# One-core linear-attention and gated-FFN kernel: the first two steps reordered, and chunk 0's first norm divided among three engines

## The reference

```
a   = layernorm(x)
q   = a @ Wq + bq                        # 16 heads of 16
k,v = (a @ Wk + bk) @ Wc @ We, (a @ Wv + bv) @ Wc @ We   # 4 heads, each used by 4 heads of q
qf, kf = elu(q) + 1, elu(k) + 1
o   = (qf . cumsum(kf v^T)) / (qf . cumsum(kf) + EPS)    # causal linear attention
y   = a + (o @ Wo + bo)                  # residual inside the attention block is a
x2  = x + (layernorm(y) * gamma + beta)  # the "first norm" of the change
z   = layernorm(x2)                      # the "second norm"
out = x2 + sigmoid(mix(z, mu_r) @ Wr^T) * (relu(mix(z, mu_k) @ Wk^T)^2 @ Wv^T)
```

## Time and profile before

| | us |
|---|---|
| median of 3 runs | 285.71 |
| lowest and highest of them | 284.47 and 287.39 |
| the profiled execution | 283.59 |
| span of the profiled execution (first to last instruction) | 281.9 |

### The profile page before, as it was taken

One profiled execution on the slowest core, in us unless ns is written; L12 is line 12 of the kernel. 1 busy time (PEld: TensorE's weight loads), 2 busy tenths in 40 slices (PEclk: granted clock), 3 DMA queues, 4 the chain that ended last, 5 costly groups with the idle time before them and its releaser, 6 DMA issues.

```text
span 281.9 us, 7526 instructions
## 1 busy us (share of the span) xinstructions
PE 262.1 (93%) x2961; PEld 188.8 (67%) x2961; DVE 219.6 (78%) x540; ACT 155.7 (55%) x316; POOL 137.9 (49%) x163
## 2 busy tenths in 40 slices
PE   7996997996999999999999999999999899979694
PEld 7854656754875688559855887568855776756573
DVE  6578576978897889798979799786979668976523
ACT  2466685595637945586448754785158610454550
POOL 2636464398851595355832585256535322242410
PEclk9799999999999999999999999999999999999999
DMA  6910220000200040002200020002000110000312
GB/s 187 257 47 1 77 78 2 3 0 2 74 3 2 2 148 3 1 3 76 77 0 2 2 76 2 2 2 77 0 2 3 40 39 0 0 2 0 113 37 74
DMA packets 12178, 10.73 MB, mean 38 GB/s; under 512 B 2288, under 2 KB 12144, under 8 KB 12144
## 3 DMA queue, kind: packets, MB, share of 16 engines
q1 hardware_dynamic: 11392, 9.97, 11.5%
q10 hardware_dynamic: 752, 0.30, 0.4%
HBM read 6.07 MB, written 4.19 MB: 36 GB/s over the span
## 4 chain that ended last, share of the span: by engine, by line
PE 80%; DVE 9%; ACT 5%; POOL 3%; issue 3%; DVEq 0%; POOLq 0%; ACTq 0%
PE ps_x L478 10%; PE ps_x L398 9%; PE ps_x L493 6%; PE ps_x L500 6%; PE ps_z L449 6%; PE ps_x L392 6%; PE ps_y L465 6%; PE ps_y L470 6%; PE ps_x L518 4%; PE ps_z L493 3%; PE ps_z L500 2%; PE ps_x L486 2%; ACT z_tok L810 2%; PE ps_z L672 2%; PE ps_x L385 2%
## 5 line engine op out<-in xcount | busy, mean ns | idle before, releaser
L1016 DVE TENSOR_TENSOR probs<-ps_z,causal 128x1024 f32<-128x1024 f32 x32 | 38.7, 1210 | 5.5 <-PE ps_z L449 4.5
L275 POOL TENSOR_TENSOR prod<-qf,ksum 128x1024 f32<-128x1024 f32 x7 | 16.6, 2365 | 32.7 <-DVE ksum L989 32.7
L478 PE MATMUL ps_x<-wo_sb,oT 128*128 128x256 f32 x128 | 29.6, 382 | 0.0
L290 POOL TENSOR_TENSOR out_tok<-tanh_r,x_tok 128x512 f32<-128x512 f32 x14 | 17.9, 1279 | 21.9 <-DVE tanh_r L1090 20.6
L398 PE MATMUL ps_x<-aT,wq_sb 128*128 128x512 f32 x60 | 27.8, 604 | 0.0
L260 POOL TENSOR_TENSOR abo_tok<-a_tok,bo_bc 128x1024 f32<-128x1024 f32 x8 | 18.9, 2361 | 16.5 <-issue 6.8
L267 POOL TENSOR_TENSOR xb_tok<-x_in,beta_bc 128x1024 f32<-128x1024 f32 x8 | 18.8, 2354 | 15.9 <-DVE x_tok L1062 15.9
L478 PEld LDWEIGHTS ps_x<-wo_sb,oT 128*128 128x128 f32 x128 | 23.6, 190 | 3.8 <-issue 0.9
L220 POOL TENSOR_TENSOR rstd<-rstd,neg_half 128x4 f32<-128x4 f32 x24 | 24.9, 1039 | 1.9
L449 PE MATMUL ps_z<-qf,kfT 32*128 32x128 f32 x512 | 23.3, 295 | 1.9 <-ACT rden_bc L730 0.5
L465 PEld LDWEIGHTS ps_y<-qf,state 32*32 32x32 f32 x512 | 11.9, 104 | 16.8 <-issue 13.9
(11 more groups left out here) (147 smaller groups left out, 615.3 us busy)
## 6 DMA issues: line engine op xcount, KB each, us to landing
x_in<-in_L_attn_x_dram SPq DMA_DIRECT2D x8, 512.0 KB, 4.3
out_dram<-out_tok SPq DMA_DIRECT2D x16, 256.0 KB, 2.2
xr<-in_L_attn_Wq_dram ACTq DMA_DIRECT2D x1, 256.0 KB, 4.1
xk<-in_L_ffn_W_r_dram SPq DMA_DIRECT2D x1, 256.0 KB, 5.0
xk<-in_L_ffn_W_k_dram SPq DMA_DIRECT2D x1, 256.0 KB, 5.2
xr<-in_L_ffn_W_v_dram SPq DMA_DIRECT2D x1, 256.0 KB, 5.7
wo_sb<-in_L_attn_Wo_dram SPq DMA_DIRECT2D x4, 64.0 KB, 5.3
bo_bc<-in_L_attn_bo_dram SPq DMA_DIRECT2D x1, 128.0 KB, 5.0
```

The lines of the kernel that those rows point to most:

```text
L478: last = mm(bk_[:, (b % 2) * D:(b % 2 + 1) * D], oT[m % 2][:, a, b, :], wo_sb[:, a, :], start=(a == 0), stop=(a == 1))
L1016: V.tensor_tensor(probs[b % 2][:].rearrange("p g (r s) -> p g r s", s=HALF), ps_z[:, :, 0:2 * P].rearrange("p g (r s) -> p g r s", s=HALF) ...
```

## The change

In steps 0 and 1, PE makes both transposes of `a`, and in step 1 the first half of the output projection, in step 0 the first FFN weight's transposes, before `spread_reciprocals`; in step 0 `keys_values` stands ahead of `scores(0, 1)` too. ACT and DVE take the matching order (`reciprocals` after `a_out(n, 1)`; `keys_values` ahead of `mask(0, 1)` in step 0).

The first norm of chunk 0 is made row by row on two ways. Rows 0 and 1: ACT normalises, POOL multiplies by gamma and adds xb. Rows 2 and 3: DVE does `centre` and `second_residual`, placed between `mask(1, 2)` and `queries(2, 0)`. `second_stats` is one call for all four rows, between `queries(2, 0)` and `queries(2, 1)`; it waits for POOL's two rows on the new semaphore s_xg. POOL makes `second_norm(0)` ahead of `denominator_terms(2)`. The wider increments of s_t and s_x2 keep the counts of the later steps as they were.

```diff
@@ -105,7 +105,7 @@
         y_tok, z_tok = sb("y_tok", NB, D), sb("z_tok", NB, D)
         stats1, mv1, rstd1 = sb("stats1", NB, 6), sb("mv1", NB, 2), sb("rstd1", NB)
         neg_mean1, nbias1 = sb("neg_mean1", NB), sb("nbias1", NB)
-        s_nb1, s_n1 = sem("nbias1_ready"), sem("y_scaled")
+        s_nb1, s_n1, s_yg, s_xg = sem("nbias1_ready"), sem("y_scaled"), sem("y_gamma"), sem("x2_by_pool")
         stats2, mv2, rstd2, neg_mean2, nbias2 = sb("stats2", NB, 6), sb("mv2", NB, 2), sb("rstd2", NB), sb("neg_mean2", NB), sb("nbias2", NB)
         zT, dz = sb("zT", KD, NB, P + 1), sb("dz", KD, NB, P)
         xk, xr = sb("xk", KD, NB, P), sb("xr", KD, NB, P)
@@ -238,15 +238,13 @@
                     pool.wait_ge(s_x2, 4 * m)
                 rstd(rstd1, mv1, s_rs1, 2 * m + 1)
 
-            def scale_residual(m):
-                for b in range(NB + 1):
-                    if b < NB:
-                        pool.wait_ge(s_n1, b + 1)
-                        PL.tensor_tensor(y_tok[:, b, :], y_tok[:, b, :], gamma_bc[:], ALU.mult).then_inc(s_t, 1)
-                    if b:
-                        pool.wait_ge(s_t, b)
-                        PL.tensor_tensor(x2_tok[m % 3][:, b - 1, :], y_tok[:, b - 1, :], xb_tok[m % 2][:, b - 1, :],
-                                         ALU.add).then_inc(s_x2, 1)
+            def scale_residual(rows):
+                for b in rows:
+                    pool.wait_ge(s_n1, b + 1)
+                    PL.tensor_tensor(y_tok[:, b, :], y_tok[:, b, :], gamma_bc[:], ALU.mult).then_inc(s_yg, 1)
+                for b in rows:
+                    pool.wait_ge(s_yg, b + 1)
+                    PL.tensor_tensor(x2_tok[0][:, b, :], y_tok[:, b, :], xb_tok[0][:, b, :], ALU.add).then_inc(s_xg, 1)
 
             def second_norm(m):
                 if m >= 1:
@@ -305,15 +303,16 @@
                 else:
                     if m >= 0:
                         scale_and_bias(m, mv1, neg_mean1, rstd1, nbias1, s_st1, s_rs1, s_nb1)
-                        scale_residual(m)
+                        scale_residual((0, 1))
                     else:
                         pool.wait_ge(s_kf, 2 * n + 2)
                     add_bo(n)
                     if m < 0:
                         add_beta(n)
+                    if m >= 0:
+                        second_norm(m)
                     denominator_terms(n)
                     if m >= 0:
-                        second_norm(m)
                         add_beta(n)
                     else:
                         pool.wait_ge(wv_split, 1)
@@ -536,23 +535,31 @@
                         pe.wait_ge(s_gt, 2 * f - 1)
                     transpose_z(f, x0, x1)
                 transpose_a(n, 0, (s_gt, 2 * f) if f >= 1 else (s_kT, 2 * c + 2))
-                pe.wait_ge(s_pr, 8 * c + 2)
-                spread_reciprocals(c, (z0, z1, z2, z3))
-                transpose_a(n, 1, (s_zT, 2 * f + 1) if f >= 0 else (s_den, c + 1))
+                if f >= 0:
+                    pe.wait_ge(s_pr, 8 * c + 2)
+                    spread_reciprocals(c, (z0, z1, z2, z3))
+                    transpose_a(n, 1, (s_zT, 2 * f + 1))
+                    pe.wait_ge(s_zT, 2 * f + 2)
+                    out_projection(m, 0, x1)
+                else:
+                    transpose_a(n, 1, (s_den, c + 1))
+                    if m >= 0:
+                        pe.wait_ge(ffn_w_sb, 3)
+                        out_projection(m, 0, x1)
+                    else:
+                        pe.wait_ge(ffn_w_in, FFN_IN)
+                        pe.wait_ge(s_qf, 2)
+                        ffn_weight(0, x1)
+                    pe.wait_ge(s_pr, 8 * c + 2)
+                    spread_reciprocals(c, (z0, z1, z2, z3))
                 if m >= 0:
-                    if f >= 0:
-                        pe.wait_ge(s_zT, 2 * f + 2)
-                    else:
-                        pe.wait_ge(ffn_w_sb, 3)
-                    out_projection(m, 0, x1)
                     pe.wait_ge(s_aT, 2 * n + 1)
                     out_projection(m, 1, x2)
-                scores(c, 1)
-                if m < 0:
-                    pe.wait_ge(ffn_w_in, FFN_IN)
-                    pe.wait_ge(s_qf, 2)
-                    ffn_weight(0, x1)
-                keys_values(n)
+                    scores(c, 1)
+                    keys_values(n)
+                else:
+                    keys_values(n)
+                    scores(c, 1)
                 if f >= 0:
                     pe.wait_ge(s_y, 2 * m + 1)
                     mix_r(f, 0, x1)
@@ -796,9 +803,9 @@
                     AC.activation(a_tok[n % 2][:, b, :], x_in[n % XBUF][:, b, :], ACT.Identity, bias=nbias0[:, b:b + 1],
                                   scale=rstd0[:, b:b + 1]).then_inc(s_a, 1)
 
-            def normalise_y(m):
-                act.wait_ge(s_nb1, 2 * m + 2)
-                for b in range(NB):
+            def normalise_y(rows):
+                act.wait_ge(s_nb1, 2)
+                for b in rows:
                     AC.activation(y_tok[:, b, :], y_tok[:, b, :], ACT.Identity, bias=nbias1[:, b:b + 1],
                                   scale=rstd1[:, b:b + 1]).then_inc(s_n1, 1)
 
@@ -841,18 +848,21 @@
                 if f >= 0:
                     shift_z(f, x0, x1)
                 a_out(n, 0)
-                reciprocals(c)
+                if f >= 0:
+                    reciprocals(c)
                 a_out(n, 1)
                 if c == 0:
                     act.wait_ge(ffn_w_ps, 1)
                     copy(flat(wrT), x1[:, :]).then_inc(ffn_w_sb, 1)
+                if f < 0:
+                    reciprocals(c)
                 if n + 1 < NC:
                     normalise_x(n + 1)
                 keys(n)
                 if f >= 0:
                     gate_r(f, 0, x1)
                 if c == 1:
-                    normalise_y(m)
+                    normalise_y((0, 1))
                 double_keys(n)
                 if f >= 0:
                     gate_r(f, 1, x2)
@@ -1045,30 +1055,31 @@
                 if i == 1:
                     row_means(stats1, mv1, s_st1, 8 * m)
 
-            def centre(m):
+            def centre(m, rows=range(NB)):
                 dve.wait_ge(s_st1, 8 * m + 8)
-                for b in range(NB):
+                for b in rows:
                     V.scalar_tensor_tensor(out=y_tok[:, b, :], in0=y_tok[:, b, :], scalar=mv1[:, b, 0:1], in1=gamma_bc[:],
-                                           op0=ALU.subtract, op1=ALU.mult).then_inc(s_t, 1)
-
-            def second_residual(m):
+                                           op0=ALU.subtract, op1=ALU.mult).then_inc(s_t, NB // len(rows))
+
+            def second_residual(m, rows=range(NB)):
                 dve.wait_ge(s_rs1, 2 * m + 2)
                 dve.wait_ge(s_xb, m + 1)
                 if m >= 3:
                     dve.wait_ge(s_out, 2 * m - 4)
                     dve.wait_ge(s_z, 4 * m - 8)
-                for b in range(NB):
-                    dve.wait_ge(s_t, 4 * m + b + 1)
+                for i, b in enumerate(rows):
+                    dve.wait_ge(s_t, 4 * m + (i + 1) * (NB // len(rows)))
                     V.scalar_tensor_tensor(out=x2_tok[m % 3][:, b, :], in0=y_tok[:, b, :], scalar=rstd1[:, b:b + 1],
-                                           in1=xb_tok[m % 2][:, b, :], op0=ALU.mult, op1=ALU.add).then_inc(s_x2, 1)
-
-            def second_stats(m, rows=range(NB)):
+                                           in1=xb_tok[m % 2][:, b, :], op0=ALU.mult, op1=ALU.add).then_inc(s_x2, NB // len(rows))
+
+            def second_stats(m):
                 if m >= 1:
                     dve.wait_ge(s_nb2, 2 * m)
-                dve.wait_ge(s_x2, 4 * m + rows[-1] + 1)
-                row_stats(x2_tok[m % 3], stats2, s_st2, 8 * m, rows)
-                if rows[-1] == NB - 1:
-                    row_means(stats2, mv2, s_st2, 8 * m)
+                else:
+                    dve.wait_ge(s_xg, 2)
+                dve.wait_ge(s_x2, 4 * m + 4)
+                row_stats(x2_tok[m % 3], stats2, s_st2, 8 * m, range(NB))
+                row_means(stats2, mv2, s_st2, 8 * m)
 
             def token_shift(m, k, dst, mu, done, read):
                 if m >= 1:
@@ -1138,22 +1149,26 @@
                 if m >= 0:
                     add_residual(m, 0, x1)
                     add_residual(m, 1, x2)
-                mask(c, 1)
-                keys_values(n)
+                    mask(c, 1)
+                    keys_values(n)
+                else:
+                    keys_values(n)
+                    mask(c, 1)
                 key_features(n)
                 divide(c, 0)
                 mask(c, 2)
+                if m >= 0:
+                    centre(m, (2, 3))
+                    second_residual(m, (2, 3))
                 queries(n, 0, x0)
                 if m >= 0:
-                    second_stats(m, (0, 1))
+                    second_stats(m)
                 queries(n, 1, x1)
```

(2 more changed lines are left out.)

## The result

| | before | after |
|---|---|---|
| median, us | 284.12 (20 runs, with the three of above) | 286.12 (20 runs) |
| lowest and highest | 282.33, 287.39 | 284.25, 287.30 |
| profiled execution (span) | 283.59 (281.9) | 286.38 (284.6) |
| mean granted clock in it | 0.994 | 0.973 |

The ratio is 1.0076, 95% interval [1.0048, 1.0105]: the change costs about 2 us, under the 1% that the prediction called no change, and clear of zero. 286.12 lies in the forecast range and 0.2 from the forecast of 285.9. That closeness is largely luck: the 285.71 I started from was the median of three runs and 1.6 too high (284.12 + 0.2 would have been 284.3), and falls of TensorE's clock, which the sum had at nothing and a rival at 0.08, put about as much on top. Every run of the kernel after has a mean granted clock of 0.988 or less.

The account below looks back on a forecast made before the run. PE was taken as the bound, without a hole from step 2's output projection to the finale. The terms -1.37 - 0.98 + 3.68 - 1.14 = +0.19, about +0.2, on 285.71 gave 285.9 us; range 282.6 to 287.6.

Parts of the forecast that it names:

- a rival at 0.08: Thinner PE work in step 1 drops the clock for 3.4 us of step 2: +1.9 us, 287.6 us, chance 0.08.
- Step 0, gain 1.37: Step 0 on PE: the reorder fills holes and starts scores(0, 2) at 30.3 instead of 31.66; bounds 1.1 to 1.64.
- Step 1's hole of 0.98: PE's wait ahead of step 1's spread is filled with second transposes and half the projection: gain 0.98 us.
- The divided norm, +2.97 at qf0: Step 1: DVE's new rows and POOL exclude each other at SBUF, residual(3) waits for add_bo; qf0 2.97 us later.
- The second order (POOL first): Variant in step 1: POOL comes first at 57.02, both residuals lie behind add_bo, same end within 0.2 us.
- Statistics between qf0 and qf1, +0.71: DVE in step 1: two more statistics rows between qf0 and qf1 add 0.67; qf1 +3.68 in all.
- The hole of 1.14 ahead of the z transposes: PE's wait for z_tok ends because the second norm comes before prod: gain 1.14 us, bounds 0.6 to 1.14.
- The sum, +0.2: All steps' gains and losses together: +0.19, say +0.2 us, for 285.9 us; the prediction's own case, chance 0.61.
- nothing else of this change can: Only the time step 2 begins on PE, at the transposes of z, reaches the end, one to one.
- no blocking: Rival: DVE's four new rows in step 1 aren't held by POOL; -2.8 us, 282.9 us, chance 0.17.
- DVE first: Rival: DVE keeps the port for its four rows in step 1, POOL waits; -2.2 us, 283.5 us, chance 0.10.
- the holes came back elsewhere: Rival: PE's holes of steps 0 and 1 return behind the next wait, up to 1.5 lost; 287.2 us, chance 0.04.

Follow-up runs that it names:

- e1: The kernel before with only the reordering of steps 0 and 1 on PE, ACT and DVE; median 281.81 us, ratio 0.9937 to before.
- e3: The changed kernel with add_bo(2) moved behind denominator_terms(2) on POOL; median 282.99 us, ratio 0.9964 to before.
- e5: The changed kernel with add_bo(2) issued as two instructions instead of one; median 285.61 us, ratio 1.0053 to before.
- e10: The changed kernel with add_bo(2) issued as four instructions instead of one; median 284.77 us, ratio 0.9993 to before.
- e11: The changed kernel with 7, 4 and 7 unused matmuls in PE's three waits of step 1; median 282.78 us, ratio 0.9961 to before.
- e4: The changed kernel with 11, 5 and 10 unused matmuls in PE's three waits of step 1; median 283.37 us, ratio 1.0003 to before.
- e7: The kernel before with only the reordering, plus 7 and 4 unused matmuls in two PE waits; median 281.37 us, ratio 0.9918 to before.

## Why the prediction was right, and where not

Times of day here are the kernel after's plus 1.06.

- **Step 0, gain 1.37.** scores(0, 2) at 30.44, predicted 30.3: the gain was 1.22, inside the bounds. PE waited 0.30 for mask(0, 1), the term that the sum had at about 0.15.
- **Step 1's hole of 0.98.** Filled; the spread at 46.06, predicted 46.1. e1 shows both gains as 2.0 to 2.5 us of time.
- **The divided norm, +2.97 at qf0.** qf0 at 59.50, predicted 59.33; a row of over 2 us beside `add_bo` (2.57), as said. The second order (POOL first) is what happened: x2 row 0 got the port, both residuals came behind `add_bo`, and the end was the same. The hold of a POOL row to 0.19 before its end fits better than the lock "for the whole instruction" of the Trainium skill ("SBUF — State Buffer", "SBUF: two separate sides"): by it qf0 would be 0.7 later by the prediction's estimate (1.0 if each of the six turns gets its 0.14 or 0.19 back), and it was 0.17 later. What the page says otherwise, that one holder excludes the other, e3, e5 and e10 bear out.
- **Statistics between qf0 and qf1, +0.71.** qf1 at 61.88, predicted 61.76. outputs(1, 3) at 66.22, predicted 66.13. PE's wait for them is 1.06 and not the 2.1 that was to show it: outputs(1, 2) ahead of them ran at the lower clock and filled the difference.
- **The hole of 1.14 ahead of the z transposes.** Gone. In e11, where the clock holds, they start at 67.43 + 1.06 = 68.49, predicted 68.5. One thing wasn't in the sum: without waiting for `z_tok` row by row they take 1.09 instead of 1.83, and PE then waits 0.69 at the spread for mask(2, 0) of the late DVE. The two cancel: the spread of step 2 is at 70.71 in e11 and at 70.52 before, +0.19.
- **The sum, +0.2.** +0.3 at clock 1.00 (e11), so the sum was right for what it summed.
- **The clock.** The step that failed is the term that the sum put at nothing: the falls of the clock, with a chance of 0.08 on the reading "1.88 did nothing". No run of the kernel after had a mean granted clock over 0.988, and in e1 the clock fell 1 us behind that very wait of 1.88. The size failed too. The rival had one stretch of 3.4 us at half clock, for 1.7 us; the profiled execution has one of 10.2 us in steps 1 and 2, which cost only 1.98, since two of the waits lie in it, and one of 3.4 us in the finale, which cost 1.70. Between the medians of the kernel after and e11 it is 3.3 us. The change shows only +2.0 because before's own median carries 1.7 us of falls (284.12 against 282.4 at clock 1.00); that +2.0 less e11's +0.3 gives the rival's 1.7 again is luck. So "nothing else of this change can" reach the end was wrong as well: the finale's fall lies behind step 2.
- **What makes it fall.** With PE's waits filled by matmuls the clock stayed up there (the profiled executions of e4, e11 and e7), so without the waits it doesn't fall. Which wait, or how thin a stretch, is not shown: in the kernel after it fell inside the second wait, before the third, and before and e1 have the same wait with PE equally busy around it, e1 with a fall and before without. I had seen the thin stretch (2.2 us of work in 8.1), compared it with one stretch that held the clock, and gave it too little. Nor had I asked what clocks the runs of before had.
- **The rivals of no blocking and of DVE first** fall by the rows of 1.03 and 2.57. That the holes came back elsewhere fell with e1.

What stays open: how the falls depend on the phase of a run. before shows clocks from 1.00 to 0.976 with one and the same program, and I tested what keeps the clock up, not what chooses the moment and the length of a fall. Nor was e7's filler tried in the prologue, where before's profile has its half clock at 10.0.

## What to carry to other kernels

An instruction moved into an engine's idle time is free only if it doesn't meet another engine at a shared port: before laying a DVE instruction with two SBUF inputs into a gap, look which POOL instruction is running there and which one is next in its queue, because the long one behind can be the one that counts. When PE's own work moves up and its feeders don't, count the work left between its waits; waits of under 2 us can cost the clock, and matmuls whose results nobody uses, no longer than the wait, buy it back (here 3.3 us of 286). Before judging a change of 1%, compare the runs of both kernels whose clock stayed at 1.00: equal means below that can hide different falls.

## What the runs showed that was not expected

- Splitting the blocking instruction in two gained nothing that could be told (1.0053 against 1.0076), because two waiting rows then each met a half; in four the median is 1.35 us lower, of which the earlier qf0 explains 1.16.
- The spread of before, 5 us, goes with the granted clock: 282.2 to 282.7 at 1.00, 283.5 to 284.1 at 0.994, 287.2 to 287.6 at 0.976. Lower mean clock isn't a time by itself: at 0.976 the kernel after takes 285.6 and before 287.4, as a fall that covers waiting costs less.
- A row of DVE beside a POOL row took 1.03 us for 0.475 of work, so a two-input norm shared by DVE and POOL at the same moment saves little: the two rows of centre took 1.90 for 0.87.
